# Reordering the second layer's linear attention in a two-layer graph kernel: q is divided before its transposes, y is accumulated transposed, and the k weights run first

## What is computed

```python
q = split_heads(x @ Wq + bq)            # x is the layer-normed input xn3
k = split_heads(x @ Wk + bk)
v = split_heads(x @ Wv + bv)
q = softmax(q, axis=-1)
k = softmax(k, axis=-1)
k_cumsum = k.sum(axis=-2, keepdims=True)
D_inv = 1.0 / (q * k_cumsum).sum(axis=-1, keepdims=True)
context = einsum('bhtd,bhte->bhde', k, v)
y = einsum('bhtd,bhde->bhte', q, context) * D_inv + q
return y @ Wp + bp
```

## Time and profile before

| | us |
|---|---|
| median of 3 runs | 756.67 |
| lowest and highest | 756.38, 757.25 |
| the profiled execution's span, first to last instruction | 755.6 |

### The profile page before, as it was taken

How to read it: one execution, slowest core, us unless ns; L and a number is a source line. 1 busy time by engine, 2 the same in 40 slices (tenths; PEclk the granted TensorE clock), 3 DMA queues, 4 the chain that set the end, 5 groups by cost and what they waited for, 6 DMA issues and landing times. The chain is left out here.

```text
span 755.6 us, 10696 instructions
## 1 busy us (share of the span) xinstructions
PE 733.0 (97%) x3884; PEld 655.2 (87%) x3884; DVE 547.4 (72%) x1071; ACT 391.2 (52%) x802; POOL 193.3 (26%) x194
## 2 busy tenths in 40 slices
PE   5999999999999999999988999999999989999998
PEld 4999888999999999988755888888888889998886
DVE  6898885654569999876878687899966776674331
ACT  5533334644748767666665464854753342553220
POOL 5358888864205520021032110000020020000000
PEclk9999999999999999999999999999999999999999
DMA  7876555436434442499453582332352363244331
GB/s 253 304 208 170 115 137 140 112 85 224 142 105 130 101 109 77 164 286 267 136 137 112 152 227 88 134 122 74 112 125 84 119 131 137 96 142 151 126 126 42
DMA packets 38532, 107.71 MB, mean 143 GB/s; under 512 B 12424, under 2 KB 12600, under 8 KB 38096
## 3 DMA queue, kind: packets, MB, share of 16 engines
q1 hardware_dynamic: 25360, 89.90, 35.4%
q0 software_dynamic: 12912, 15.00, 12.5%
q10 hardware_dynamic: 208, 2.12, 0.8%
HBM read 96.31 MB, written 2.83 MB: 131 GB/s over the span
## 5 line engine op out<-in xcount | busy, mean ns | idle before, releaser
L1263 DVE TENSOR_TENSOR w_lo<-raw,w_hi 128x1024 fp32r<-128x1024 f32 x140 | 170.0, 1222 | 71.1 <-ACT w_hi L955 70.7
L955 ACT ACTIVATE w_hi<-raw 128x1024 fp32r<-128x1024 f32 x140 | 147.5, 1057 | 102.3 <-PE bank L1970 81.1
L1918 PE MATMUL bank<-xn1T,w_hi 128*128 128x384 f32 x416 | 106.1, 335 | 0.0
L1970 PE MATMUL bank<-w_hi,xn3T 128*128 128x512 f32 x288 | 92.6, 394 | 0.0
L816 POOL DMA_INDIRECT count_table<-total,place x48 | 82.9, 1727 | 26.5 <-issue 14.3
L1918 PEld LDWEIGHTS bank<-xn1T,w_hi 128*128 128x128 f32 x416 | 74.9, 188 | 0.1
L1918 PE MATMUL bank<-xn1T,w_lo 128*128 128x384 f32 x208 | 69.5, 334 | 0.0
L1970 PEld LDWEIGHTS bank<-w_hi,xn3T 128*128 128x128 f32 x288 | 54.1, 188 | 11.0
L816 POOL DMA_INDIRECT mask_table<-value,place x48 | 54.1, 1126 | 31.0 <-issue 13.1
L1918 PE MATMUL bank<-xn4T,w_hi 128*128 128x384 f32 x240 | 61.1, 335 | 0.0
L1970 PE MATMUL bank<-w_lo,xn3T 128*128 128x512 f32 x144 | 56.0, 389 | 0.0
(11 more groups left out here) (353 smaller groups left out, 1682.7 us busy)
## 6 DMA issues: line engine op xcount, KB each, us to landing
raw<-weights SPq DMA_DIRECT2D x140, 512.0 KB, 3.6
row_sb<-rows SPq DMA_DIRECT2D x6, 512.0 KB, 6.0
kcat<-kcat POOLq DMA_DIRECT2D x16, 192.0 KB, 2.9
base<-rows POOLq DMA_DIRECT2D x6, 512.0 KB, 13.0
w1r<-w_in ACTq DMA_DIRECT2D x1, 2048.0 KB, 8.8
w2r<-w_in SPq DMA_DIRECT2D x1, 2048.0 KB, 10.3
x_sb<-x_in SPq DMA_DIRECT2D x3, 512.0 KB, 5.0
row_sb<-rows SPq DMA_DIRECT2D x6, 256.0 KB, 5.1
```

The lines of the kernel that those rows point to most:

```text
L955: act.activation(w_hi[:, u % RING], raw[:, u % RAW], ACT.Copy).then_inc(hi_split, 1)
L1263: dve.tensor_tensor(w_lo[:, u % RING], raw[:, u % RAW], f(w_hi[:, u % RING]), ALU.subtract).then_inc(unit_split, 1)
L1918: last = pe.matmul(out_of(pr)[:, 0:N], w[pa][:, slot, k * P:(k + 1) * P], TT[src][:, pb, k], start=(k == 0 and m == 0), stop=(k == KD - 1 ...
L1970: last = pe.matmul(out_of(pr)[:], tile[:, pa, k, ts], w[pb][:, at_, j * HALF:(j + 1) * HALF], start=(kk == 0 and j == 0 and m == 0 and nam ...
```

## The change

1. **Order.** In each half the units run k, q, v instead of q, k, v, and the softmax steps of k and q change places.
2. **Denominator.** A new step `key_sum` (PE) multiplies a matrix of ones by both parts of `k2n`: six products of 512 columns into bank 7. A new step `divide` (DVE), one per tile of 128 nodes, multiplies q by it, sums each head, takes the reciprocal and writes the divided q to `qd`. `queries` transposes `qd` instead of q. v loses its columns of ones.
3. **Context.** High and low part of v lie side by side in `v_parts`, so the high part of k meets both in one product of 256 columns; the low part of k meets the high part of v in one of 128. DVE adds the two column blocks.
4. **y.** For each chunk PE transposes plain q into a bank and accumulates context-transposed times `q1T` (three products of 384 columns) onto it. The result is already transposed; `transpose_y` and DVE's division of y are gone.
5. **Places.** `queries` of the first half moves to after units 13 and 14 (it was after 10 and 11), the second of them directly behind `context`; in the second half both stand around the first `wp` units. Zeroing of the second half's context moves to POOL.

The diff, cut to its core:

```diff
+    after = {1: [("degree",), ("hop_dot", 0)], 2: [("norm",)], 3: [("hop_row", 0), ("hop_mul", 0)], 4: [("hop_msg", 0), *exps("k", 0, 0)],
+             5: [*exps("k", 0, 1), *ends("k", 0, 0)], 6: [("hop_sum", 0), *exps("k", 0, 2), *ends("k", 0, 1), ("hop_dot", 1)],
+             7: ends("k", 0, 2), 8: [("hop_row", 1), *exps("q", 0, 0), ("key_sum", 0), ("hop_mul", 1)],
+             9: [("hop_msg", 1), *exps("q", 0, 1), *ends("q", 0, 0), ("divide", 0, 0)],
+             10: [*exps("q", 0, 2), *ends("q", 0, 1), ("divide", 0, 1)],
+             11: [("hop_sum", 1), *ends("q", 0, 2), ("divide", 0, 2)], 12: [("hop_dot", 2)],
+             13: [("queries", 0)],
+             14: [("context", 0), ("queries", 1), ("hop_row", 2), ("hop_mul", 2)], 15: [("hop_msg", 2), ("y", 0)],
+             16: [("y", 2), *exps("k", 1, 0), ("hop_sum", 2)],
+             17: [*exps("k", 1, 1), *ends("k", 1, 0), ("hop_dot", 3)],
+             18: [*exps("k", 1, 2), *ends("k", 1, 1)],
+             19: [*ends("k", 1, 2), ("hop_row", 3), ("hop_mul", 3)], 20: [("hop_msg", 3), ("key_sum", 1), *exps("q", 1, 0)],
+             21: [*exps("q", 1, 1), *ends("q", 1, 0), ("divide", 1, 0)],
+             22: [*exps("q", 1, 2), *ends("q", 1, 1), ("divide", 1, 1), ("hop_sum", 3)],
+             23: [*ends("q", 1, 2), ("divide", 1, 2)]}
-        for name in ("q", "k", "v"):
+        for name in ("k", "q", "v"):
...
-    steps.extend([("part", 0, 1, "wp", 4), ("context", 1)])
+    steps.extend([("queries", 2), ("part", 0, 1, "wp", 4), ("queries", 3), ("context", 1)])
     run("wp", 4, 5)
-    steps.extend([("y", 1, 0), ("part", 0, 2, "wp", 1), ("y", 1, 2)])
+    steps.extend([("part", 0, 2, "wp", 1), ("y", 4)])
     run("wp", 1, 2)
-    steps.extend([("part", 0, 1, "wp", 5), ("transpose_y", 2), ("part", 1, 2, "wp", 5), ("transpose_y", 3)])
+    steps.append(("y", 6))
...
+        elif kind == "key_sum":
+            product(f"key_sum.{s[1]}", 7)
...
+                if kind == "divide":
+                    _, c, t = s
+                    sl = slice(c * HALF, (c + 1) * HALF)
+                    pr = f"key_sum.{c}"
+                    wait_full(dve, pr)
+                    dve.wait_ge(q_ready, sub_no("q", c, t))
+                    ins = dve.tensor_tensor(kq[:], qf[:, t, sl], out_of(pr)[:], ALU.mult)
...
+                    link(dve.tensor_reduce(den[:, t], heads(kq[:]), X, ALU.add))
+                    link(dve.reciprocal(den[:, t], den[:, t]))
...
+                    dve.tensor_tensor(heads(qd[:, t]), heads(qf[:, t, sl]), bcast(den[:, t], [P, HALF // DH, DH]),
+                                      ALU.mult).then_inc(divided, 1)
...
+                if kind == "key_sum":
+                    pr = f"key_sum.{s[1]}"
+                    pe.wait_ge(node_split, 2 * NT * (s[1] + 1) + NT)
+                    pe.wait_ge(v_ones, 1)
+                    wait_bank(pe, pr)
+                    for t, part in [(t, part) for t in range(NT) for part in (HI, LO)]:
+                        last = pe.matmul(out_of(pr)[:], ones_r[:], k2n[:, part, t], start=(t == 0 and part == HI),
+                                         stop=(t == NT - 1 and part == LO))
+                    full(last, pr)
...
                             for t in range(NT):
-                                pe.matmul(o, k2n[:, HI, t, js], v_hi[:, t, j], start=(t == 0), stop=False)
-                                pe.matmul(o[:, 0:P], k2n[:, HI, t, js], v_lo[:, t, j], start=False, stop=False)
-                                last = pe.matmul(o, k2n[:, LO, t, js], v_hi[:, t, j], start=False, stop=(t == NT - 1))
+                                pe.matmul(o, k2n[:, HI, t, js], v_parts[:, t, j].rearrange("p a c -> p (a c)"),
+                                          start=(t == 0), stop=False)
+                                last = pe.matmul(o[:, 0:P], k2n[:, LO, t, js], v_parts[:, t, j, 0], start=False,
+                                                 stop=(t == NT - 1))
...
                 if kind == "queries":
-                    pe.wait_ge(q_ready, sub_no("q", s[1] // 2, NT - 1))
+                    pe.wait_ge(divided, NT * (s[1] // 2 + 1))
                     for j in range(2 * s[1], 2 * s[1] + 2):
-                        transposes(f"q1T.{j}", [qf[:, t, j * P:(j + 1) * P] for t in range(NT)])
+                        transposes(f"q1T.{j}", [qd[:, t, j % KH * P:(j % KH + 1) * P] for t in range(NT)])
                 if kind == "y":
...
+                        for t in range(NT):
+                            pe.matmul(out_of(pr)[:, t * P:(t + 1) * P], qf[:, t, k * P:(k + 1) * P], ident[:],
+                                      is_transpose=True, start=(t == 0), stop=False, skip_group_check=True)
+                        for m, (pa, pb) in enumerate(PASSES):
+                            last = pe.matmul(out_of(pr)[:, 0:N], ctx1[c][:, pa, j], TT["q1T"][:, pb, j], start=False,
+                                             stop=(m == 2), skip_group_check=True)
```

More of the change, by code:

```diff
@@ L190, in ends @@
         return [("soft_end", name, c, t) for t in tiles]
[L192 to L204, removed]
@@ L387, in plan_banks @@
         elif kind == "y":
-            for b in range(s[2], s[2] + 2):
-                product(f"yn.{s[1]}.{b}", 6 + b % 2)
+            for k in range(s[1], s[1] + 2):
+                product(f"y.{k}", 6 + k % 2)
         elif kind == "gate":
@@ L1017, in _ @@
                         split_up_to(AHEAD - 1)
[L1018 to L1021, removed]
+                if kind == "y":
+                    for k in range(s[1], s[1] + 2):
                         chunk_hi("y", k, f"y.{k}")
@@ L1504, in _ @@
                                 else:
[L1505 removed]
+                                    low, high, src = v_parts[:, t, :, 1], v_parts[:, t, :, 0], v_both[:, t, :, 1]
                                 lo_part(low, src, high).then_inc(node_split, 1)
@@ L1860, in _ @@
                             full(last, pr)
-                if kind == "transpose_y":
-                    pe.wait_ge(y_ready, (NT + 1) * (s[1] // 2 + 1))
-                    for k in range(2 * s[1], 2 * s[1] + 2):
-                        transposes(f"y.{k}", [qf[:, t, k * P:(k + 1) * P] for t in range(NT)])
+                if kind == "key_sum":
[7 more added lines that the diff above has]
+                    full(last, pr)
                 if kind == "degree":
@@ L2163, in _ @@
-                    for b in range(2):
-                        wait_emptied(pe, f"context.{c}.{b}")
-                    wait_emptied(pe, f"q1T.{4 * c + 2}")
-                    wait_emptied(pe, f"q1T.{4 * c + 3}")
-                    for b in range(s[2], s[2] + 2):
-                        pr = f"yn.{c}.{b}"
-                        wait_bank(pe, pr)
-                        for n in range(3):
-                            t, j = (b, n) if b < NT else (n, 3)
-                            last = products(out_of(pr)[:, 130 * n:130 * n + 130],
-                                            [(lambda p: TT["q1T"][:, p, j, t * P:(t + 1) * P], lambda p: ctx1[:, p, KH * c + j])])
+                    c = s[1] // KH
@@ new lines, in _ @@
+                    for k in range(s[1], s[1] + 2):
+                        pr, j = f"y.{k}", k % KH
+                        wait_emptied(pe, f"context.{c}.{j // 2}")
+                        wait_emptied(pe, f"q1T.{k}")
+                        wait_bank(pe, pr)
+                        for t in range(NT):
[4 more added lines that the diff above has]
+                                             stop=(m == 2), skip_group_check=True)
```

107 lines of the change are left out of this document (48 added, 59 removed).

## The result

The changed kernel takes **769.32 us** (median of five runs, 768.20 to 773.85) against 756.67 (five runs, 756.21 to 757.25): a ratio of 1.0179, 95% interval 1.0162 to 1.0196 (estimated from all runs; the two medians alone give 1.0167). It is slower, as forecast, but by 12.7 us where 9.1 were forecast. It lies at the edge of the range: by the median just inside (769.3 against 770.0), by the ratio just outside (756.67 x 1.0179 = 770.2). The profiled execution took 771.99 with a span of 770.2; by span it stands 14.6 above the kernel before.

What follows compares the result with a forecast made beforehand. The prediction took TensorE (PE), busy 97% of the span, as the bound, with VectorE's and ScalarE's queues deciding whether its new waits are covered. Stalls of 12.5 us less 3.4 saved gave +9.1: 756.7 to 765.8 us, range 758.5 to 770.

Steps and rivals of the forecast that it cites:

- The waits: New TensorE stalls in both halves, from VectorE and ScalarE data or banks coming late; 12.5 us in all.
- 1.9, 2.7, 3.5 and 1.7: First-half stalls of TensorE in us: at `hop_row` 1, `key_sum` 0, `context` 0 and `queries` 1.
- 1.2, 0.4 and 1.1: Second-half stalls of TensorE in us: at `key_sum` 1, `queries` 3 and `context` 1.
- The fourth: At `queries` 1, directly behind `context` 0: TensorE waits for the same banks, 6 and 7, to be emptied; 1.7 us.
- 16.0 us of VectorE behind `hop_sum` 1: VectorE's queue up to q1T's split, against 12.95 us of TensorE work; with 0.4 restart, 3.5 lost at `context` 0.
- TensorE's saving: Key sums, context, queries and y: TensorE's work falls by 1.7 us a half, 3.4 in all.
- The rival in which the wide product doesn't pay: At the context: 256 columns cost two narrow products, the 24 cost 2.5 us more; 768.3 us, chance 0.07.
- The 3.4: TensorE's work saved over both halves, in us, subtracted from the stalls.
- The sum: Whole kernel: stalls of 12.5 us less 3.4 saved give +9.1, so 765.8 us; chance 0.61.
- DVE catching up: Rival: VectorE catches up before `context` 0, whose 3.5 us stall goes; 762.3 us, chance 0.18.
- The clock: Rival: half rate for a unit after each of the two longest pauses adds 2 x 4.1 us; 774, chance 0.04.

Runs made afterwards that it cites:

- k_filled: The changed kernel with products that nobody reads put ahead of three of TensorE's waits; 765.32 us, ratio 1.0115 to the kernel before.
- f_narrow: The changed kernel with steps of both halves moved and each 256-column context product cut into two of 128; 762.24 us, ratio 1.0074 to the kernel before.
- a: The changed kernel with `hop_dot` 1 ahead of k's exponentials and division of tile 1; 768.74 us, ratio 1.0154 to the kernel before.
- b: As `a`, with `key_sum` 0 and the first division of q one unit later; 767.21 us, ratio 1.0132 to the kernel before.
- l: The changed kernel with steps of both halves moved and ScalarE's second-hop message copies ahead of its copy of k's last split; 758.84 us, ratio 1.0027.
- h_pause6: The kernel before with TensorE waiting ahead of the second row step for six unused GpSimd operations; 763.30 us, ratio 1.0087.
- h_pause2: The kernel before with TensorE waiting ahead of the second row step for two unused GpSimd operations; 758.40 us, ratio 1.0024.
- d_all: The changed kernel with the edits of `b`, and in the first half `hop_dot` 2, `context` 0 and `y` later, `queries` 1 ahead of `context` 0; 761.38 us, ratio 1.0051.
- g_order_alone: The kernel before with its own arithmetic, k units ahead of q and steps placed as in the change; 767.73 us, ratio 1.0161.

## Why the prediction was right and wrong

**The waits, right.** Forecast 1.9, 2.7, 3.5 and 1.7; measured idle time 1.52, 2.49, 3.45 and 1.28. In the second half 1.2, 0.4 and 1.1 against 0.73, no wait, and 0.94. Together 12.5 against 10.4 of idle time. The forecast counts from start to start, with the restart; so counted, the first three are 468.84 - 467.16 = 1.68, 472.27 - 469.53 = 2.74 and 508.68 - 505.06 = 3.62 in `k_filled`. The fourth is forecast as a wait for both banks, one after the other. Behind the context at half rate only one of them was left (1.28); at full clock, in `k_filled`, both are there, 0.78 and 0.67. The terms that the prediction writes down for it end at 4.6 - 3.5 = 1.1; they reach its 1.7 only with restarts that it doesn't write down. The method that gave the waits was to add up the queue of VectorE, instruction by instruction, from the last point at which TensorE had released it. The longest queue, 16.0 us of VectorE behind `hop_sum` 1, gave 3.5 against 3.45 of idle time and 3.62 from start to start.

**TensorE's saving, right.** The one price without a row, 256 columns, was taken at 0.12 between two rows; a pair with 128 columns then costs 0.231, and at 589 us the pairs start 0.23 apart. The time of `f_narrow` fits it. The rival in which the wide product doesn't pay falls. The 3.4 as a whole was not measured by itself.

**The sum, right as far as it went.** +9.1 forecast; `k_filled`, which keeps the clock, gives +8.8. The whole, +12.7, lies 3.6 above the sum, and that is about what the clock costs.

**DVE catching up, wrong as a rival.** I gave it 0.18. The stall at `context` 0 is the longest of all, and `a`, `b` and `l` show the other face of it: VectorE has no air there to catch up in.

**The clock, the step that failed.** The sum puts the clock at nothing and its chance at 0.04, because TensorE had idled 5.8 us once with every slice at full clock. The runs showed half rate behind the waits of 2.49 and 3.45, about 4 us in all. Neither row carries the reason against it, and where the 5.8 lie the prediction doesn't say. Here they are, in the kernel before: TensorE's timeline from the start, then 24 transposes of the same form in two stretches (count, busy time, mean ns of one), then the stretch with the granted clock of the first.

```profile
9.42 4.91 PE L1858 MATMUL bank<-ident,xn_nat 128*128 128x128 f32 x21 [5.78 <-ACT xn_nat L995]
...
L1858 PE MATMUL bank<-ident,xn_nat 128*128 128x128 f32 x24 | 5.5, 427 | 5.8 <-ACT xn_nat L995 5.8
L1858 PE MATMUL bank<-ident,xn_nat 128*128 128x128 f32 x24 | 3.4, 279 | 1.6 <-DVE xn_nat L1293 1.0 <-DVE x_sb L1521 0.6
...
9.40:11.00 1.60, 1.58 (x7) 1.36 (x7) 0.85 (x3) 1.26 (x2) 0.86 (x3) 1.00 0.97 378
```

The 5.8 us are the start of the program, when TensorE had done one transpose. And the products behind them did run slowly: 427 ns each, where 24 such transposes took 279 around 610 us. That is the pace of the half rate: the six transposes of the row step take 443 ns each behind the pause of `h_pause6`, at clock 0.50, and 287 behind that of `h_pause2`, at 1.00. The clock's column says 1.00 over the transposes at 9.42 all the same. So full slices were no evidence against the rival. The durations don't show either that the 5.8 us lowered the clock, since nothing there shows that it had been up before; they only take the reason against the rival away. The rule of the Trainium skill ("TensorE: Matmul & The Clock Gate", Why this matters for your kernels) that I set aside, idle gaps put TensorE back to half rate, agrees with `h_pause6` (4.75 us, clock 0.50) and with the changed kernel (2.49 and 3.45); the 2.63 of `f_narrow` shows that not every such gap does it. The Trainium skill ("TensorE: Matmul & The Clock Gate", Seeing it yourself) also says that the record of the clock's changes is not to be fully trusted, which the row of 9.40 agrees with.

Its price in the forecast, a unit at half rate behind each of the two longest pauses (+8.2), was too high: 2.1 behind the pause of 4.75 in `h_pause6`, and about 4 in all in the changed kernel (769.32 less 765.32). With hindsight, had the rival been taken for the forecast at that price, it would have been 765.8 + 4 = 769.8.

**What stays open.** Which pauses cost clock. In the profiled executions of all the kernels here, 13 of the 14 pauses of 2.49 us or more between 455 and 620 us are followed by a clock below 1; the fourteenth is the 2.63 of `f_narrow`, while 2.63 in `d_all` did cost clock. By themselves, pauses of 1.90 or less were followed by no fall, but for that in `f_narrow`; 1.76 in ten runs of `h_pause2` cost nothing beyond its length. But `g_order_alone`, with no profiled pause above 1.5, lost 0.007 of the clock in two runs of four, which were not the profiled one. So the same kernel loses clock in one run and not in another, for a reason that no run here shows. The changed kernel's own runs spread by 5.7 us where those of before spread by 1.0.

## What to carry to other kernels

When TensorE is the bound and a change makes it wait, add to each wait of some microseconds the half rate that may follow it (it followed 13 of 14 waits of 2.5 us and more here): about a third of the loss came on top of the waits, and even products that nobody reads were worth 4 us in their place. Before setting that aside because the clock's row is full, compare the duration of one and the same instruction behind a pause and far from one. And where a step's inputs pass through a second engine that is nearly full, moving the step trades one wait for another; sum that engine's queue up to the point at which the data are wanted, as the waits here were forecast, and look for a place with less ahead of it.

## What the runs showed of the hardware

- A pause of 4.75 us on TensorE, alone, put its granted clock to 0.50 (1.2 GHz) from the end of the pause at 472 to about 478 us (`h_pause6`): products of 512 columns 0.43 apart in place of 0.23. After a pause of 1.76 it stayed at 1.00 (`h_pause2`). Products that nobody reads, put into three waits, kept it at 1.00 (`k_filled`).
- The clock also fell in the middle of a run of narrow products, 2.7 us after the last of two pauses of 0.95 and less (`f_narrow`, 513.9 us).
- At the start of the program the granted clock's column shows 1.00 over transposes that take 427 ns each, where they take 279 around 610 us (kernel before).
- A product of 256 columns followed by one of 128: the next pair starts 0.23 us later (changed kernel, 589 us). Three narrow products (128 or 130 columns, 0.111 each) take 0.33 (kernel before).
